# One bank for g1, two shared by output and prediction: re-dividing PSUM and re-ordering all engines in a two-layer cross-attention kernel

## The reference, cut to what matters

```python
# layer 0, per sequence: x (256x512), c (256x256)
Q = x @ Wq0 + bq0;  K = c @ Wk0 + bk0;  V = c @ Wv0 + bv0
x1 = x + softmax(Q @ K.T * scale, over keys) @ V @ Wo0 + bo0
# layer 1, with x1 in place of x: softmax over the QUERY axis
q = x1 @ Wq1 + bq1;  k = c @ Wk1 + bk1;  v = c @ Wv1 + bv1
w = softmax(q @ k.T / sqrt(512), axis=query);  pred = w @ v
x2 = pred + x1
out = (x2 - mean) * rsqrt(var + 1e-6) * gamma + beta
```

## Time and profile before

| | us |
|---|---|
| median of 3 runs (1397.57 to 1401.15) | 1397.83 |
| the profiled execution, its own time | 1400.27 |
| span of its trace | 1398.5 |
| mean from one E_blk to the next, sequences 3 to 63 | 20.42 |

### The profile page before, as it was taken

One profiled execution on the slowest core, in us unless ns is written; L12 is line 12 of the kernel. 1 busy time (PEld: TensorE's weight loads), 2 busy tenths in 40 slices (PEclk: granted clock), 3 DMA queues, 4 the chain that ended last, 5 costly groups with the idle time before them and its releaser, 6 DMA issues.

```text
span 1398.5 us, 25082 instructions
## 1 busy us (share of the span) xinstructions
PE 1203.5 (86%) x7985; PEld 1092.3 (78%) x7985; DVE 1161.8 (83%) x2125; ACT 757.2 (54%) x1608; POOL 955.9 (68%) x708
## 2 busy tenths in 40 slices
PE   6979888888988988899898898888889888888973
PEld 5768777887877877788888888788878877787873
DVE  0348898898898889888888888988988888898874
ACT  1436655655565565565556556556555655655542
POOL 2436677677767767777776776777777777677755
PEclk9989999999999999999999999999999999999997
DMA  7335565566556556565565565655555565565441
GB/s 301 112 128 175 170 193 186 191 186 188 189 167 191 191 172 196 187 188 179 188 195 163 186 195 167 197 188 183 189 187 187 170 191 193 180 198 188 139 119 60
DMA packets 131839, 250.09 MB, mean 179 GB/s; under 512 B 15712, under 2 KB 89440, under 8 KB 123232
## 3 DMA queue, kind: packets, MB, share of 16 engines
q1 hardware_dynamic: 130800, 248.64, 56.2%
q10 hardware_dynamic: 1008, 1.06, 0.2%
HBM read 165.68 MB, written 83.95 MB: 179 GB/s over the span
## 4 chain that ended last, share of the span: by engine, by line
DVE 45%; issue 27%; ACT 14%; PE 8%; DMA 3%; POOL 2%; DVEq 1%; ACTq 0%; SPq 0%; POOLq 0%
DVE junk L755 11%; PE bank L299 7%; DVE stats L833 6%; DVE bank L819 4%; ACT yT_hi L491 4%; ACT E L533 4%; DVE R L739 4%; DVE scol L810 4%; DVE w_lo L790 3%; DVE uT_lo L705 3%; ACT w_hi L491 2%; DVE nmax L776 2%; DVE vT_lo L698 2%; DVE wcT_lo L698 2%; DVE y_blk L747 1%
## 5 line engine op out<-in xcount | busy, mean ns | idle before, releaser
L940 POOL TENSOR_TENSOR yT_lo<-yT_raw,yT_hi 128x1024 fp32r<-128x1024 f32 x64 | 153.2, 2394 | 170.8 <-ACT yT_hi L491 170.8
L299 PE MATMUL bank<-xT_hi,A_hi 128*128 128x256 f32 x512 | 155.8, 304 | 118.6 <-DVE scol L810 118.6
L755 DVE SCALAR_TENSOR_TENSOR junk<-R,g_b 128x512 f32<-128x512 f32 x128 | 224.9, 1757 | 0.0
L491 ACT ACTIVATE bank<-gT 128x512 f32<-128x512 f32 x64 | 38.5, 602 | 309.9 <-DMA gT<-g_dram 308.3
L299 PEld LDWEIGHTS bank<-xT_hi,A_hi 128*128 128x128 f32 x512 | 103.0, 201 | 129.2 <-issue 103.0
L940 POOL TENSOR_TENSOR xT_lo<-IN,xT_hi 128x1024 fp32r<-128x1024 f32 x64 | 158.7, 2480 | 27.9 <-ACT xT_hi L491 27.9
L299 PE MATMUL bank<-yT_hi,A_hi 128*128 128x256 f32 x512 | 150.6, 294 | 30.7 <-POOL yT_lo L940 30.7
L988 POOL TENSOR_TENSOR Y<-Y,gamma_b 128x512 f32<-128x512 f32 x128 | 173.6, 1378 | 2.7 <-ACT Y L613 2.7
L613 ACT ACTIVATE Y<-bank,nmr,rstd 128x512 f32<-128x512 f32 x128 | 92.8, 776 | 134.8 <-POOL nmr L980 134.8
L991 POOL TENSOR_TENSOR Y<-Y,beta_b 128x512 f32<-128x512 f32 x128 | 163.3, 1296 | 0.0
L819 DVE SCALAR_TENSOR_TENSOR bank<-bv_b,scol,R 128x512 f32<-128x512 f32 x128 | 155.3, 1256 | 2.6 <-ACT Y L613 2.6
(11 more groups left out here) (107 smaller groups left out, 4297.5 us busy)
## 6 DMA issues: line engine op xcount, KB each, us to landing
IN<-in_packed SPq DMA_DIRECT2D x64, 1024.0 KB, 5.8
R<-in_x SPq DMA_DIRECT2D x64, 512.0 KB, 3.4
y_dram<-y_blk SPq DMA_DIRECT2D x256, 128.0 KB, 2.3
yT_raw<-y_dram SPq DMA_DIRECT2D x64, 512.0 KB, 4.3
out<-Y SPq DMA_DIRECT2D x64, 512.0 KB, 5.0
E_dram<-E_blk SPq DMA_DIRECT2D x256, 64.0 KB, 3.7
PT_raw<-E_dram SPq DMA_DIRECT2D x64, 256.0 KB, 2.7
gT<-g_dram SPq DMA_DIRECT2D x64, 128.0 KB, 5.7
```

What stands on the lines that cost most here:

```text
L299: last = nc.tensor.matmul(dst, stat(a, t), mov(b, t), start=(not seeded and t == 0 and n == 0), stop=(t == k - 1 and n == 2), skip_group_c ...
L491: return nc.scalar.activation(dst, src, ACT.Copy, **kw)
L755: nc.vector.scalar_tensor_tensor(junk[q][:, :], R[n.k % 4][:, q, :], 1.0, g1_b[:, :], ALU.mult, ALU.mult, accum_out=gcol[:, q, 0:1]).then_ ...
L940: return nc.gpsimd.tensor_tensor(dst, src, fp(hi), ALU.subtract)
```

## The change

1. **PSUM.** g1 stays in bank 3, where its product put it. out and pred of one row half share a bank (6 and 7). s has bank 0 for itself, so `u_` no longer waits for `s_set`.
2. **pred_seed** moves from DVE to ACT and writes s * bv1 only. x1 is added afterwards by a new DVE operation `x2` (PSUM + SBUF to R in SBUF). moments and normalise read R in SBUF instead of the bank.
3. **w_low_sum** moves from DVE to POOL, at the end of its body.
4. **Waits.** `out_seed_(r+2)` waits for `x2_set(r-1)` (the bank must be free), `pred_seed_` for `x1_set(r+1)`, `load_x` for `Y_set` (R is read until normalise), `wc_` for `w_lo`. SP's `move_E0` and `move_y` are cut into a write and a read part with `store` between `write_E0` and `read_E0`.
5. **Orders** of the bodies of all five engines are new.
6. The products of the weights at the start use other banks.

```diff
-        out_bank = (bank[0], bank[3])
+        s_bank = bank[0]
         Pc_bank = v_bank = bank[1]
-        u_bank = s_bank = bank[2]
+        u_bank = bank[2]
+        g1_b = bank[3]
         S0_bank = wc_bank = bank[4]
         S1_bank = bank[5]
-        pred_bank = bank[6:8]
+        out_bank = pred_bank = bank[6:8]
...
             def load_x(n):
-                first(sp, pred_seed, n.count(2, 1, back=4))
+                first(sp, Y_set, n.count(2, 1, back=4))
...
             def body(r):          # SP
+                load_x(r.plus(2))
                 write_g(r.plus(1))
-                load_x(r.plus(2))
                 load_IN(r.plus(5))
                 read_g(r.plus(1))
-                move_E0(r.plus(3))
-                move_y(r.plus(2))
+                write_E0(r.plus(3))
                 store(r.plus(-2))
+                read_E0(r.plus(3))
+                write_y(r.plus(2))
+                read_y(r.plus(2))
...
             def u_(n):
                 pe.wait_ge(xT_lo, n.count())
                 first(pe, u_lo, n.count(2, 1, back=1))
-                first(pe, s_set, n.count(back=4))
...
             def s_(n):
-                if n.plus(3).there():
-                    pe.wait_ge(u_lo, n.plus(3).count(2, 1))
-                else:
-                    pe.wait_ge(s_set, n.count(back=1))
+                first(pe, s_set, n.count(back=1))
                 pe.wait_ge(w_los_set, n.count())
...
             def wc_(n):
+                pe.wait_ge(w_lo, n.count())
...
             def body(r, u=True):  # PE
                 if u:
                     u_(r.plus(3))
-                S1_(r)
-                Pc_(r.plus(2))
-                S0_(r.plus(3))
                 pred_(r.plus(-1), 0)
                 pred_(r.plus(-1), 1)
+                Pc_(r.plus(2))
+                S1_(r)
+                S0_(r.plus(3))
                 out_(r.plus(2), 0)
                 out_(r.plus(2), 1)
                 v_(r.plus(1))
+                wc_(r)
                 s_(r)
-                wc_(r)
...
             def out_seed_(n):     # ACT
                 for q in range(ST):
                     first(act, x1_set, n.count(2, q, back=1))
+                    first(act, x2_set, n.count(2, q, back=3))
                     copy(out_bank[q][:, :], c1_b[:, :], scale=Z0[:, q:q + 1]).then_inc(out_seed, 1)
+
+            def pred_seed_(n):    # ACT
+                if not n.there():
+                    return
+                act.wait_ge(s_set, n.count())
+                for q in range(ST):
+                    if n.plus(2).there():
+                        act.wait_ge(x1_set, n.plus(2).count(2, q))
+                    else:
+                        act.wait_ge(x2_set, n.count(2, q, back=1))
+                    copy(pred_bank[q][:, :], bv1_b[:, :], scale=scol[:, q, 0:1]).then_inc(pred_seed, 1)
...
             def body(r, prefix=True):  # ACT
                 if prefix:
                     wc_h(r.plus(-1))
+                    pred_seed_(r.plus(-1))
+                    PT_h(r.plus(2))
                     u_h(r.plus(3))
                     C_h(r.plus(3))
                 xT_h(r.plus(4))
                 if prefix:
                     out_seed_(r.plus(2))
+                Pc_h(r.plus(2))
+                yT_h(r.plus(1))
                 exps1(r)
-                Pc_h(r.plus(2))
+                exps0(r.plus(3))
                 w_h(r)
-                yT_h(r.plus(1))
-                exps0(r.plus(3))
-                S1_seed_(r.plus(1))
-                v_h(r.plus(1))
                 cT_h(r.plus(4))
                 normalise(r.plus(-1))
-                PT_h(r.plus(3))
+                v_h(r.plus(1))
+                S1_seed_(r.plus(1))
...
-            def pred_seed_(n):    # DVE
-                dve.wait_ge(s_set, n.count())
-                for q in range(ST):
-                    first(dve, Y_set, n.count(2, q, back=1))
-                    nc.vector.scalar_tensor_tensor(pred_bank[q][:, :], bv1_b[:, :], scol[:, q, 0:1],
-                                                   R[n.k % 4][:, q, :], ALU.mult, ALU.add).then_inc(pred_seed, 1)
...
+            def x2(n, q):         # DVE
+                if not n.there():
+                    return
+                dve.wait_ge(pred_full, n.count(2, q))
+                nc.vector.tensor_tensor(R[n.k % 4][:, q, :], pred_bank[q][:, :], R[n.k % 4][:, q, :], ALU.add
+                                        ).then_inc(x2_set, 1)
...
             def body(r, u=True):  # DVE
+                wc_l(r.plus(-1))
                 dot(r.plus(1), 0)
-                pred_seed_(r.plus(-1))
-                wc_l(r.plus(-1))
+                dot(r.plus(1), 1)
+                g_blocks(r.plus(1))
+                x2(r.plus(-1), 0)
                 if u:
                     u_l(r.plus(3))
+                x2(r.plus(-1), 1)
+                moments(r.plus(-1))
+                Pc_l(r.plus(2))
                 max1(r)
-                dot(r.plus(1), 1)
-                g_blocks(r.plus(1))
+                max0(r.plus(3))
                 rz1_(r)
-                Pc_l(r.plus(2))
-                max0(r.plus(3))
+                stats_ready(r.plus(-1))
                 E0_blocks(r.plus(3))
+                variances(r.plus(-1))
+                x1(r.plus(2), 0)
                 w_l(r)
-                w_low_sum(r)
-                moments(r.plus(-1))
-                stats_ready(r.plus(-1))
-                x1(r.plus(2), 0)
                 x1(r.plus(2), 1)
                 y_blocks(r.plus(2))
-                variances(r.plus(-1))
+                v_l(r.plus(1))
                 s_columns(r)
-                v_l(r.plus(1))
...
             def body(r, prefix=True):  # POOL
+                finish(r.plus(-2))
                 if prefix:
                     PT_l(r.plus(2))
                     C_l(r.plus(3))
                 xT_l(r.plus(4))
                 yT_l(r.plus(1))
-                finish(r.plus(-2))
                 scales(r.plus(-1))
                 cT_l(r.plus(4))
+                w_low_sum(r)
```

More of the change, by code:

```diff
@@ L217, in move_E0, with read_E0, write_y @@
                                  ).then_inc(E0_out, 16)
+            def read_E0(n):
+                if not n.there():
+                    return
                 sp.wait_ge(E0_out, n.count(64, 63))
                 sp.dma_start(flat4(PT_raw), E0_dram.rearrange("a m i x -> (a m) (i x)")).then_inc(PT_in, 16)
-            def move_y(n):
+            def write_y(n):
                 if not n.there():
@@ L263, in _ @@
             load_IN(Seq(2))
-            move_E0(Seq(0))
+            write_E0(Seq(0))
+            read_E0(Seq(0))
             load_IN(Seq(3))
-            move_E0(Seq(1))
+            write_E0(Seq(1))
+            read_E0(Seq(1))
             load_IN(Seq(4))
-            move_y(Seq(0))
-            move_E0(Seq(2))
+            write_y(Seq(0))
+            read_y(Seq(0))
+            write_E0(Seq(2))
+            read_E0(Seq(2))
             write_g(Seq(0))
             read_g(Seq(0))
-            move_y(Seq(1))
+            write_y(Seq(1))
+            read_y(Seq(1))
             def body(r):
+                load_x(r.plus(2))
                 write_g(r.plus(1))
-                load_x(r.plus(2))
                 load_IN(r.plus(5))
                 read_g(r.plus(1))
-                move_E0(r.plus(3))
-                move_y(r.plus(2))
+                write_E0(r.plus(3))
                 store(r.plus(-2))
+                read_E0(r.plus(3))
+                write_y(r.plus(2))
+                read_y(r.plus(2))
             for r in range(0, LOOP_FROM):
@@ L436, in _ @@
             pe.wait_ge(w_in[3], 16)
-            over_h(bank[0][:, :], lambda h: WvT0_s[:, h, 0:P], Wo0_s)
-            over_h(bank[3][:, :], lambda h: WvT0_s[:, h, P:2 * P], Wo0_s)
+            over_h(bank[6][:, :], lambda h: WvT0_s[:, h, 0:P], Wo0_s)
+            over_h(bank[7][:, :], lambda h: WvT0_s[:, h, P:2 * P], Wo0_s)
             S0_(Seq(0))
             u_(Seq(1))
-            over_h(bank[7][:, :], wide(1), Wo0_s)
+            over_h(bank[0][:, :], wide(1), Wo0_s)
             pe.wait_ge(w_in[4], 16)
@@ L445, in _ @@
             S0_(Seq(1))
-            over_h(bank[6][:, :], wide(2), WqT1_s)
+            over_h(bank[3][:, :], wide(2), WqT1_s)
             Pc_(Seq(0))
             u_(Seq(2))
-            pe.wait_ge(su_lo, 5)
             out_(Seq(0), 0)
             out_(Seq(0), 1)
-            pe.wait_ge(su_lo, 7)
-            A_half(bank[5], WqT1_s, WkT1_s, 1)
+            pe.wait_ge(su_lo, 6)
+            A_half(bank[0], WqT1_s, WkT1_s, 1)
             Pc_(Seq(1))
@@ L578, in out_seed_ @@
                     first(act, x1_set, n.count(2, q, back=1))
+                    first(act, x2_set, n.count(2, q, back=3))
                     copy(out_bank[q][:, :], c1_b[:, :], scale=Z0[:, q:q + 1]).then_inc(out_seed, 1)
+            def pred_seed_(n):
+                if not n.there():
+                    return
+                act.wait_ge(s_set, n.count())
```

(27 more changed lines are left out.)

19 lines of the change are left out of this document (8 added, 11 removed).

## The result

The changed kernel takes 1211.01 us (median of 4 runs, 1209.69 to 1213.19), 0.866 of the time before (95% interval 0.864 to 0.869). The span of its profiled execution is 1207.9 us. 1229 was forecast, with 1208 to 1300 as its range: the measured time lies near the lower end.

The account below looks back on a forecast made before the run. PE's own work was taken as the bound: 17.5 us a body plus 0.2 for near loops, 17.7. From 1398.5, 60 x (20.42 - 17.7) = 163 and 6 for the tail came off: 1229 us, range 1208 to 1300.

Parts of the forecast that it names:

- The bound: PE, back to back, needs 17.5 us a body; before, DVE's order set 20.42 and PE waited for s_columns.
- The POOL way: Loop from Pc through E_blk, variances, scales, cT_lo, w_low_sum, finish and PT_lo to the next Pc: 17.2 us, below PE's 17.5.
- E0 way: Loop from Pc through E_blk, E0's DMA write and read, PT_h and PT_lo to the next Pc: 14.6 us, or 16.4.
- u's wait: PE's wait before u for DVE's s_columns goes, as s has its own bank: worth up to 2.9 us a body.
- What two inputs in SBUF cost: Three such DVE operations lose time to POOL; where POOL is idle, the first takes 0.68 us and the third 0.42.
- dot: On DVE, with g1 in PSUM, dot takes 0.75 us instead of 1.76: 2.0 us of DVE less a body.
- pred_seed and w_low_sum: Moved off DVE: -1.1 and -1.4 us there; ACT gains 2 x 0.65 to 0.69, POOL 0.7.
- SP's order: SP's DMA issues: read_E0 behind store, write_y behind read_E0; g's seed on ACT last, at 16.3 us; all covered.
- Rival 1: A loop binds, the POOL way at its upper ends being 18.5 us: 18.6 us a body, 1283 us; chance 0.24.
- Rival 2: Shared PSUM banks stall the orders, x2 late by 3 us, PE losing 1.8: 19.4 us a body, 1331; chance 0.10.
- Rival 3: dot gains nothing from g1 in PSUM, DVE's first part grows by 2.0: about 19.0 us a body, 1307; chance 0.06.
- Rival 4: E0's read waits until the store has landed, 5.0 us more: 21.4 us a body, 1452, slower than before; chance 0.04.

Follow-up runs that it names:

- run 8: Changed kernel with pred's product of high wcT with low V1 left out, 8 matmuls a body in place of 12: 1188.45 us, 16.99 us a body.
- run 1: Changed kernel, but u waits again until DVE has read the sum s of the body before: 1298.75 us, 18.83 us a body.
- run 2: Changed kernel, but g1 lies in SBUF again, so dot has two inputs there: 1242.1 us, 17.89 us a body.
- run 3: Changed kernel, but the low parts of w are summed on DVE again, right after w_l: 1213.01 us, 17.41 us a body.
- run 12: Changed kernel, but pred's seed is written by DVE, with one input in SBUF, and not by ACT: 1213.54 us, 17.36 us a body.
- run 5: Kernel before the change, with only the low-part sum of w moved from DVE to POOL: 1337.35 us, 19.48 us a body.
- run 7: Changed kernel with two more operations like w_low_sum on POOL in each body, output read by nobody: 1272.71 us, 18.37 us a body.
- run 4: Changed kernel, but PE runs pred after S0 as before, and DVE takes u_l ahead of x2: 1609.78 us, 23.91 us a body.
- run 11: Changed kernel, but SP issues the read of E0 ahead of the store of Y: 1212.31 us, 17.36 us a body.

## Why the prediction was right, step by step

- **The bound.** PE's need was worked out as 17.5 and is 17.36. The terms as written add up to 17.6; u's 2.93 held the start after a wait (u takes 2.86 back to back). The comparison with the kernel before was weaker than it looks: it took off 2.4 us, the longest wait, from the mean body, and the mean wait of 2.0 leaves 18.4. The 0.2 us that I allowed for near loops was not needed.
- **The error.** The bodies gave 0.34 us x 60 = 20 us more than forecast, the tail 2 (7.8, forecast 6), and the start took 0.8 back: 21 us for the span, 1229 against 1207.9. The median of the runs lies 3.1 us above that span, where I had it 0.7 below, so it is off by 18 only. The range was lucky in this: its lower end stood for 17.4 us a body, the kernel runs at 17.36, and the span of the profiled execution lies 0.1 us under 1208.
- **The POOL way.** 17.2 forecast, 16.99 measured in run 8. The term that was too high is finish, 5.3, now 5.0 us (2.50 and 2.51). In the E0 way the terms add up to 14.9 and 16.5 us, not 14.6 and 16.4; nothing hung on it. Loops near a bound cost nothing until they pass it.
- **u's wait.** Right and necessary (run 1): 1.47 us a body, as u then stands for the 1.2 us of the wait and its hand-offs.
- **What two inputs in SBUF cost.** The second row was misread, by the text and by its heading: POOL's yT_lo starts at 1340.61, 0.08 us behind the sum's 0.42 us operation, and is 0.2 us longer than its mean. So that operation didn't run beside an idle POOL, it came first. The first row holds: POOL is idle from 1335.23 to 1340.61.
- **dot.** Direction right, 0.75 forecast, 0.68 found. Its own part in the end is 0.53 us a body (run 2), not 2 us: DVE's time is no longer what is short, and what remains is POOL's loss.
- **pred_seed and w_low_sum.** Sizes about right (0.68 on ACT, 0.74 on POOL). That they change engines is worth nothing in the new kernel (runs 3, 12); in the old one the second brings 60 us (run 5). The Trainium skill (Perfetto Trace Analysis, Optimizing Scalar/DVE Operations) says that moving work between DVE and GpSimd might not help. Run 5 did it in the old kernel and gained 60 us; in the new one it is worth 2 us (run 3), with PE as the bound.
- **SP's order.** E0's read is issued 3.1 us after its writes (602.91 to 606.03 in the timeline), not the 4.71 of the loop before, and 1.1 us after the store's issue (604.95), not some 3; the store lands after 2.6 us, not 5.0. Before, a load of IN was issued at 726.92, 3.2 us ahead of E0's writes at 730.16, and IN takes 5.8 us to land (median); now it is issued at 735.72, 6.1 us ahead of those at 741.79, and takes 4.9. That this is the reason was not tried.
- **Rival 1** (a loop binds) is refuted for this kernel by 0.37 us a body. In runs 2, 7 and 8 the loop binds; at its own work it is 16.99 us long, not the 18.5 of the upper ends.
- **Rival 2** (the shared banks stall the orders): the cover holds, so refuted. Run 4 shows the mechanism at 2.9 us once pred is moved next to out. The Trainium skill (Perfetto Trace Analysis, Matmul Optimizations) has the rule that all 8 PSUM banks be put to work for parallelism. Here two banks do the work of four and PE waits for neither, with 4.3 us of other products between pred and out; run 4 shows what it costs without them.
- **Rival 3** (dot gains nothing) is refuted by the 680 ns, and its price of 19.0 us was too high: 17.89 in run 2. It counted DVE's time and left out that covers absorb it; what PE waits for in run 2 is POOL's PT_lo.
- **Rival 4** (E0's read behind the store) is refuted by run 11.
- POOL was forecast at 88% busy and is 87% in the window and 80% in the span. The DMA share was forecast at 64% and the page has 61.6% in the main queue.

## What to carry to other kernels

Add up each engine's work for one body at the rate at which it runs back to back, and then the length of every chain that leads from a body to the next: the time is the longest of all these, and an operation that is moved changes only the chains that it leaves and enters. When two users of one resource are to share it, put as much other work between them in the order as the hand-over takes; the same operations 4 us apart cost nothing, and side by side more than the whole gain. Where GpSimd's chain is near the bound, put one of the two inputs of a VectorE operation beside it into PSUM: here that was worth 31 us (run 2). An operation with both inputs in SBUF that stands where there is room costs 2 us at most (run 3).

## What I had not expected of the hardware

Two operations that meet at SBUF both get longer: in run 2 dot by 0.79 us, and beta and PT_lo on POOL by 0.21 and 0.41 on average, and it was POOL's part that set the time. And a stall can cost TensorE twice. In run 4, with two stalls of 2.9 and 1.6 us a body, the granted clock is 0.93 on average over 800 us, that is it was at 1.2 GHz for about a seventh of the time (an estimate from the two levels). It fell behind the longer stall in the body shown, and not behind the shorter one. In run 1 one stall of 1.2 us a body left it at 1.00, and in the kernel before, with one of 2.0 on average and up to 2.4, it is 0.98.
